# A cross-attention and FFN kernel: the output projection of a head pair as seven block products

## The reference

```
q, k, v = LN(x) @ Wq, ctx @ Wk, ctx @ Wv        # 16 heads of 128, scaled
x = x + softmax(q k^T) v @ Wo                   # Wo is 2048 x 512
x = x + down(silu(gate(n)) * up(n)), n = LN(x)  # 512 -> 2048 -> 512
```

## Time and profile before

| | us |
|---|---|
| median of 3 runs | 2033.76 (2032.74 to 2034.96) |
| the profiled execution | 2033.7 |
| its span | 2032.1 |
| PE busy | 2015.9 |
| DVE busy | 1528.7 |
| ACT busy | 1001.7 |
| POOL busy | 733.0 |

### The profile page before, as it was taken

How to read it: one execution, slowest core, us unless ns; L and a number is a source line. 1 busy time by engine, 2 the same in 40 slices (tenths; PEclk the granted TensorE clock), 3 DMA queues, 4 the chain that set the end, 5 groups by cost and what they waited for, 6 DMA issues and landing times.

```text
span 2032.1 us, 44899 instructions
## 1 busy us (share of the span) xinstructions
PE 2015.9 (99%) x15422; PEld 1509.0 (74%) x15422; DVE 1528.7 (75%) x3346; ACT 1001.7 (49%) x2679; POOL 733.0 (36%) x872
## 2 busy tenths in 40 slices
PE   8999999999999999999999999999999999999999
PEld 6888888788888887878888888888888885444444
DVE  6767777777777777777787777776666557899886
ACT  8955554554555545554555555554555443333332
POOL 5422232332333233333332323322111104877776
PEclk9999999999999999999999999999999999999999
DMA  8834444444444444444444343534332364555555
GB/s 255 217 65 90 83 97 87 84 92 92 88 88 91 92 91 86 88 89 91 89 89 92 77 105 73 104 74 91 55 82 58 68 136 97 91 89 94 92 91 99
DMA packets 456112, 193.75 MB, mean 95 GB/s; under 512 B 419456, under 2 KB 432256, under 8 KB 455904
## 3 DMA queue, kind: packets, MB, share of 16 engines
q1 hardware_dynamic: 433984, 140.31, 36.2%
q0 software_dynamic: 15584, 44.45, 8.8%
q10 hardware_dynamic: 6336, 6.29, 1.0%
HBM read 61.21 MB, written 27.26 MB: 44 GB/s over the span
## 4 chain that ended last, share of the span: by engine, by line
PE 93%; DVE 2%; DMA 2%; ACT 2%; issue 1%; DVEq 0%; SPq 0%; POOL 0%; ACTq 0%; POOLq 0%
PE b_qk L1103 33%; PE b_v L1103 17%; PE b_c L1103 10%; PE b_s L1103 9%; PE b_w L1158 8%; PE b_o L1158 8%; PE b_o L1229 3%; PE b_w L1229 2%; PE b_x L1103 2%; PE b_pt L1103 2%; DMA probT<-psplit 1%; DMA attn_weights<-wattn 0%; ACT psplit L665 0%; DVE nmax L919 0%; ACT prob L655 0%
## 5 line engine op out<-in xcount | busy, mean ns | idle before, releaser
L1103 PE MATMUL b_qk<-kvT,attn_weights 128*128 128x256 f16 x3072 | 377.2, 273 | 3.5 <-DVE qk L757 2.5
L1103 PE MATMUL b_qk<-xT,attn_weights 128*128 128x256 f16 x3072 | 377.2, 273 | 0.0
L1103 PE MATMUL b_v<-attn_weights,kvT 128*128 128x256 f16 x3072 | 377.2, 273 | 0.0
L655 ACT ACTIVATE prob<-b_s,nmax 128x256 f32<-128x256 f32 x514 | 239.2, 470 | 274.8 <-DVE nmax L919 272.8
L1103 PEld LDWEIGHTS b_qk<-kvT,attn_weights 128*128 128x128 f16 x3072 | 300.3, 98 | 92.5 <-issue 3.5
L946 DVE SCALAR_TENSOR_TENSOR psplit<-prob,rrec,psplit 128x256 f16<-128x256 f32 x514 | 307.1, 638 | 79.1 <-ACT psplit L665 79.1
L611 ACT ACTIVATE qk<-b_qk 128x512 f16<-128x512 f32 x256 | 152.5, 596 | 428.1 <-PE b_qk L1103 428.0
L757 DVE SCALAR_TENSOR_TENSOR qk<-b_qk,qk 128x512 f16<-128x512 f32 x256 | 176.7, 690 | 247.7 <-ACT qk L611 240.0
L1103 PEld LDWEIGHTS b_qk<-xT,attn_weights 128*128 128x128 f16 x3072 | 300.6, 98 | 34.8
L1103 PEld LDWEIGHTS b_v<-attn_weights,kvT 128*128 128x128 f16 x3072 | 300.6, 98 | 34.8
L665 ACT ACTIVATE psplit<-prob,rrec 128x256 f16<-128x256 f32 x514 | 233.1, 500 | 67.5 <-DVE rrec L939 67.5
(11 more groups left out here) (137 smaller groups left out, 2678.4 us busy)
## 6 DMA issues: line engine op xcount, KB each, us to landing
ffn_w<-wffn SPq DMA_DIRECT2D x48, 256.0 KB, 2.9
acc<-xtok POOLq DMA_DIRECT2D x16, 512.0 KB, 4.7
out<-acc POOLq DMA_DIRECT2D x16, 512.0 KB, 3.3
xrow<-xtok POOLq DMA_DIRECT2D x31, 256.0 KB, 3.2
kvrow<-kvt POOLq DMA_DIRECT2D x61, 128.0 KB, 2.4
out<-attn_weights POOLq DMA_DIRECT2D x28, 256.0 KB, 5.3
stage<-wattn SPq DMA_DIRECT2D x12, 512.0 KB, 4.5
ffn_scratch<-ffn_t SPq DMA_DIRECT2D x48, 128.0 KB, 1.9
```

The lines of the kernel that those rows point to most:

```text
L655: last = eng.activation(half(prob, q, 256), half(bS, q, 256), ACT.Exp, bias=nmax[:, q:q + 1], scale=1.0, accum_out=rsum[:, q:q + 1])
L1103: last = eng.matmul(out, l, r, start=(a == 0), stop=(a == len(pairs) - 1))
```

## The change

From element 2 on, the projection of a pair of heads is made by blocks. The left side is a 2 x 2 of blocks (two row tiles by two heads), the right side is a 2 x 2 (two heads by two halves of the columns). Seven products of sums of such blocks take the place of eight. Elements 0 and 1 keep the old form.

- ACT evicts contexts as float32 (`evict_rows`); POOL forms five sums in three instructions (`left_sums`); ACT writes the seven rounded blocks (`left_hi`) and DVE the remainders (`left_lo`).
- `project_fast` multiplies a pair in two steps, four terms and then three, each of three 256-column matmuls, into seven half banks (`b_pt`, `b_x`, `b_o`, `b_w`) that collect over the eight pairs. DVE adds them to `acc` in twelve additions of 256 columns (`add_products`), four in each of three steps of the next element's first quad; PE waits for them through `READ` before it opens a half bank again.
- The sums of Wo's blocks are made and split once, in element 1 (`load_out`, `out_sums`, `out_hi`, `out_sums_hi`, `out_lo`, `store_out`), and kept in DRAM. Two of eight pairs' blocks stay in SBUF, six are loaded for every element through two slots (`load_slot`), by SP, whose loop over the quads is now written out.
- The FFN weights' quantisation begins an element later, at quad 8.
- Of a tile's inverse root POOL keeps only the power (`tile_power`); DVE does the rest (`x1_aggr`, `x1_root`). Statistics move from the first quad's third and fourth step to the second quad's second.
- In the last stage the last element's twelve additions stand behind pairs 0, 1 and 2, four each; the third gate and up bank is used from chunk 6 on; the last element's other steps come ten pairs later; six pairs after the first four are without a down product, and ten halves are made behind the last pair. The buffers of the stage lie elsewhere.

```diff
-FFN_FROM, FFN_TO = QPB, QPB + FFN_TILES
+FFN_FROM, FFN_TO = 2 * QPB, 2 * QPB + FFN_TILES
...
-NO_DOWN = (0, 1, 2, 3, 36, 40, 44, 48)
+NO_DOWN = (0, 1, 2, 3, 44, 47, 50, 53, 56, 59)
...
-GU_BUF = [u % 2 if u < 4 else (u - 2) % 3 for u in range(2 * PAIRS)]
+THIRD = 6
+LAST_BEHIND = (None, None, None, 2, 1, None, 4, 6, 7, 5, 3, 10)
+GU_BUF = [u % 2 if u < THIRD else (u - THIRD + 2) % 3 for u in range(2 * PAIRS)]
...
+LEFT = {"a0": 0, "b1": 1, "a0+b1": 2, "a0+b0": 3, "a1+b1": 4, "b0-b1": 5, "a0-a1": 6}
+TERMS = (("m1", "a0+b1", 3), ("m3", "a0", 2), ("m4", "b1", 1), ("m2", "a1+b1", 0)), \
+    (("m6", "a0-a1", 5), ("m5", "a0+b0", 4), ("m7", "b0-b1", 6))
+READ = {"m1": 4, "m3": 4, "m4": 8, "m2": 8, "m6": 9, "m5": 12, "m7": 12}
...
+            def store_out(j):
+
+                eng.wait_ge(sm["wo_lo"], j + 1)
+                eng.dma_start(wos[PREP[j]], wo_split).then_inc(sm["wo_stored"], 16)
...
+            def left_sums(n, k):
+
+                wait_apart(eng, "c_hi", 4 * n + k + 1)
...
+                eng.tensor_tensor(blocks[:, 4:6, :], blocks[:, 1:9:7, :], blocks[:, 0:4:2, :], ALU.add
+                                  ).then_inc(sm["s_sum"], 1)
+                eng.tensor_tensor(blocks[:, 6:8, :], blocks[:, 0:2, :], blocks[:, 2:9:6, :], ALU.subtract
+                                  ).then_inc(sm["s_sum"], 1)
+                eng.tensor_tensor(blocks[:, 3, :], blocks[:, 1, :], blocks[:, 2, :], ALU.add).then_inc(sm["s_sum"], 1)
...
+            def left_hi(n, k):
+
+                u = 2 * n + k // 2 - 2 - FAST_PAIR
+                eng.wait_ge(sm["s_sum"], 3 * (u + 1))
...
+                eng.activation(left_part(k // 2, 0).rearrange("p (n f) -> p n f", f=P), blocks[:, 1:8, :], ACT.Copy,
+                               scale=1.0).then_inc(sm["s_hi"], 1)
...
+            def left_lo(n, k):
+
+                eng.wait_ge(sm["s_hi"], 2 * n + k // 2 - 1 - FAST_PAIR)
+                eng.tensor_tensor(left_part(k // 2, 1).rearrange("p (n f) -> p n f", f=P), blocks[:, 1:8, :],
+                                  left_part(k // 2, 0).rearrange("p (n f) -> p n f", f=P), ALU.subtract
+                                  ).then_inc(sm["s_lo"], 1)
...
+            def add_product(b, name, sign, tile_, side, behind):
+
+                if behind is not None:
+                    eng.wait_ge(sm["m_step"], 12 * (b - FAST) + behind)
+                a = acc[:, bass.ds(((b + 1) & 1) * (2 * D) + tile_ * D + side * 256, 256)]
+                eng.scalar_tensor_tensor(out=a, in0=product_at[name], scalar=sign * O_OUT, in1=a, op0=ALU.mult,
+                                         op1=ALU.add).then_inc(sm["m_step"], 1)
...
+                    sums = q == 1 and (not isinstance(s, int) or s > FAST)
+                    if sums and k > 0:
+                        add_products(s - 1, k - 1)
+                    if q == 2 and k == 1 and (not isinstance(s, int) or s > 0):
+                        for j in range(2):
+                            x1_stats(s - 1, j)
+                        x1_aggr(s - 1)
+                    if q == 2 and k == 2 and (not isinstance(s, int) or s > 0):
+                        x1_root(s - 1)
...
+                if v < 3:
+                    for at in range(4 * v, 4 * v + 4):
+                        add_last(at)
...
+                if u == THIRD:
+                    eng.wait_ge(sm["m_step"], 12 * (B - 1 - FAST) + 8)
...
+            def project_fast(u, part):
+
+                batch, first_, last_ = u // 8, u % 8 == 0, u % 8 == 7
+                slot, use = slot_use(u)
+                eng.wait_ge(sm[f"slot_loaded{slot}{part}"], 16 * use)
+                if part == 0:
+                    eng.wait_ge(sm["s_lo"], u - FAST_PAIR + 1)
...
+                for name, rows, block_ in TERMS[part]:
+                    at = LEFT[rows] * P
+                    if first_ and batch > FAST:
+                        eng.wait_ge(sm["m_step"], 12 * (batch - 1 - FAST) + READ[name])
+                    for z, (a, b) in enumerate(PARTS):
+                        last = eng.matmul(product_at[name], left_part(u % 2, a)[:, at:at + P], slot_w(slot, block_, b),
+                                          start=(first_ and z == 0 and name in OPENS), stop=(last_ and z == len(PARTS) - 1 and name in CLOSES))
+                last.then_inc(sm["o_done"], 1)
```

More of the change, by code:

```diff
@@ L260, in qk_part, with fast @@
             return qk[:, at:at + 512]
+        def fast(n, k, lead):
+            return not isinstance(n, int) or 4 * n + k - lead >= FAST_HEAD
         def head_slot(k):
@@ L337, in odd @@
-            def odd(n):
-                return (n - 1) // 2 if n % 2 and n < NQ - 4 else None
-            for n in range(QPB):
-                for k in range(QUAD):
-                    transpose_p(4 * n + k, k % 2)
-                    if n % 2 and k == 1:
-                        transpose_x(n // 2)
-                    for g in (EARLY + PIECES * n + 2 * k, EARLY + PIECES * n + 2 * k + 1):
-                        if PIECES <= g < QPB * PIECES - SLOTS:
-                            reload(g)
@@ L366, in load_x_tile @@
                                         ).then_inc(sm[f"xqT_loaded{at}"], 16)
-            for n in range(NQ - 4, NQ - 1):
-                ffn_quad(n, store=False, load=False)
-            for k in range(QUAD):
-                transpose_p(4 * (NQ - 1) + k, k % 2)
-                if k < 2:
-                    load_x_tile(k, k)
+            begin = {0: 2 * 1 + 6, 4: 2 * 3 + 6, 1: 2 * 5 + 6, 2: 2 * 6 + 6}
+            fills = {}
+            for p_, step in begin.items():
+                for part in range(2):
+                    fills.setdefault(FAST_HEAD - 16 + step + part, []).append((FAST_PAIR + p_, part, FAST_HEAD - 20 + step))
@@ new lines, in out_lo @@
+            def out_lo(j):
+                eng.wait_ge(sm["wo_hi"], 2 * j + 2)
+                to, hi_part = wo_part(1), wo_part(0)
+                pairs = [(to[:, 0:5:4, :], wo_rows[:, 0:4:3, :], hi_part[:, 0:5:4, :])]
+                for a in range(2):
+                    at = slice(1 + 4 * a, 3 + 4 * a)
+                    pairs.append((to[:, at, :], wo_sums[:, 2 * a:2 * a + 2, :], hi_part[:, at, :]))
+                pairs.append((to[:, 3, :], wo_cross, hi_part[:, 3, :]))
+                for dst, rows, above in pairs:
+                    last = eng.scalar_tensor_tensor(out=dst, in0=rows, scalar=W_SCALE, in1=above,
+                                                    op0=ALU.mult, op1=ALU.subtract)
+                last.then_inc(sm["wo_lo"], 1)
@@ L929, in quad @@
                         kv_lo(n)
-                    if ffn and k == 2:
+                    if ffn and k == 2 + sums:
                         ffn_magic(w)
@@ L1209, in _ @@
                 quad(n)
-            for n in range(FFN_FROM, NQ):
+            for n in range(QPB, NQ):
                 if n <= NQ - 4:
```

421 lines of the change are left out of this document (291 added, 130 removed).

## The result

| | before | after |
|---|---|---|
| median, us | 2033.87 (2032.74 to 2034.96, 5 runs) | 2042.87 (2042.58 to 2044.32, 5 runs) |
| the profiled execution | 2033.7 | 2043.3 |
| its span | 2032.1 | 2041.5 |

The ratio is 1.0046, with a 95% interval of 1.0031 to 1.0060: the changed kernel is 0.5% slower. 2025 us were forecast, faster; the sign is wrong, and the time lies near the upper end of the range. The granted TensorE clock was 1.000 of full speed in both kernels, so no part of the difference is the clock's.

What follows compares the result with a forecast made beforehand. TensorE, busy 99%, was taken to bound the kernel. 2033.7 - 35.7 + 15.6 + 3.5 + 4 + 1 + 5 = 2027.1, less 2 for shared stalls, gave 2025 us; range 2010 to 2044.

Steps and rivals of the forecast that it cites:

- The saving: Projection of a head pair: 21 products of 256 columns replace 12 of 512, 0.32 us for each of 112 pairs, -35.7 us.
- The boundary: First steps of the next element: PE waits for DVE's additions before reopening banks, 1.2 us per element, +15.6 us (6.5 to 29).
- Where DVE fills up: Third step of a quad: new remainder and moved root meet tile normalisation, 0.3 us stall in 11 elements, +3.5 us (0 to 14).
- the second rival: Spread stalls where DVE's new remainder meets POOL's sums or roundings: 0.15 us or more per pair turns the sign; chance 0.18.
- Element 1: Splitting the sums of Wo's blocks through one staging buffer, with store and load in turn, +4 us (0 to 16).
- Slot loads: Six of eight weight blocks reloaded for each element on SP, 672 KB every two steps, +1 us (0 to 6).
- The end: End of attention and last stage: last pairs' chain and twelve additions ahead of the first chunks, +5 us (2 to 10).
- The 2 us taken off for shared stalls: In the sum: a PE stall gives DVE back time it lacks in the next step, so 2 us were deducted.
- A chain that ends at 9.6 us: A pair's evictions, sums, blocks and remainders: DVE ends near 9.6 us, 8 us before the product, so hidden.

Runs made afterwards that it cites:

- the small remainder: The changed kernel with DVE making the remainder of one of the seven left blocks, six left out: 2022.90 us, ratio 0.9941.

## Why the prediction was wrong

- **The saving** was computed at 0.32 us per pair, 35.7 in all; measured 6.54 + 6.54 - 6.55 - 6.22 = 0.31 per pair, and some 33.4 between the step starts (the last three pairs lie behind them, in the end). The mechanism held.
- **The boundary**: forecast 1.2 us per element, 15.6; measured 0.97, 12.6. Place, wait and cause are as described (0.3 forecast for the first of the two steps, 0.32 measured); this step is right.
- **Where DVE fills up is the step that failed.** It was costed at 0.3 us in 11 elements, 3.5 us, with an upper bound of 14. Measured: 1.02 us in the 12th step and up to 0.51 in the 14th, which had no term, over 12 elements: 15.5 us, above the bound. The sum put the new remainder (1.08) and the root (0.5) on top of a qk remainder whose place was taken from the earlier trace rows, and so let the rest of DVE's row stay where it was. In fact the reciprocal came 1.25 us later against the step's start (0.42 ahead to 0.83 behind). Of that, 0.59 is the root (0.99 from 713.50 to 714.49, less 0.33 for the context remainder that went and 0.07 of small differences), near the 0.5 forecast. The other 0.66 is the row maximum, which starts 4.81 us into the step before in place of 4.13 (that step is 0.02 longer), and had no term. The prediction had read 1.58 us of idle time in that very step as DVE's room. They are gone: the moved statistics hold DVE from 707.39 to 709.25, and the qk remainder starts 4.21 us into the step in place of 3.45. The statistics aren't enough by themselves: with the small remainder, which also shortens DVE's row in the 10th step, the row maximum is at 4.13 again with the statistics where they are. No run moved them back. 1.25 + 1.0 for the remainder take the qk remainder's end from 4.84 us of the earlier trace rows to 7.09, where 6.5 was forecast. PE follows 0.15 us later, which was not counted either, in a step of 6.22. The whole stall is 1.02.
- **Contention was priced in the wrong sentence.** That POOL holds DVE's two-input remainders was seen in the earlier trace rows, and the second rival had its mechanism and its place (where the remainder meets sums or roundings), with a chance of 0.18 and a loss for each pair. The loss came only in the two steps beside the roundings: 12.7 us, against the 17 at which the rival was to turn the sign. Sums of POOL between them cost nothing that PE sees. By its own sign (waits on the qk remainder of tens of us) this rival came true in part: 20.3 us. In the trace of before the two remainders already took 2.08 us; that was paid from DVE's idle time, and the change used this up. The Trainium skill (GPSIMD Engine Reference, Key points) names the contention for instructions with two SBUF inputs; the runs agree: 2.12 us beside the roundings, 0.88 apart from them.
- **Element 1**: forecast +4, measured +4.7; the load behind the store on SP's queue is 4.0 of it by the two traces compared, 2.2 by the average of all.
- **Slot loads**: forecast +1; the waits on transposes are 1.3 us in place of 2.9. No cost, although a pair's loads are 896 KB (512 and 384 in the view of DMA issues) and not the 672 of the prediction.
- **The end**: forecast +5, measured +7.0. 5.5 of it up to the last matmul, in stalls at the places described. In size two differ: pair 127's remainder makes PE wait 1.01 (0.5 forecast), pair 126's 0.3 (0.8 forecast). The kernel after, PE:

```profile
1698.86 1.02 PE L1354 MATMUL b_s<-attn_weights,out_weights 128*128 128x512 bf16 x4 [0.57 <-ACT cbuf L770]
1703.48 0.82 PE L1415 MATMUL b_pt<-out_weights,stage 128*128 128x256 f16 x6 [1.01 <-DVE stage L1084]
1708.54 1.02 PE L1354 MATMUL b_qk<-attn_weights,out_weights 128*128 128x512 bf16 x4 [0.87 <-DVE attn_weights L987]
1713.41 1.04 PE L1354 MATMUL b_pt<-attn_weights,out_weights 128*128 128x512 bf16 x4 [1.26 <-DVE acc L1107]
1719.84 1.04 PE L1354 MATMUL b_pt<-attn_weights,out_weights 128*128 128x512 bf16 x4 [1.08 <-DVE attn_weights L987]
```

  They answer to the one 0.83 of the earlier trace rows. The other 1.5 us are behind the last matmul, and were not forecast: the last stores take longer to land. The views of DMA issues of before and of after (count, KB, median us to landing):

```profile
out<-acc SPq DMA_DIRECT2D x4, 256.0 KB, 3.2
```

```profile
out<-acc SPq DMA_DIRECT2D x4, 256.0 KB, 4.8
```

  Why they do was not tried, and stays open, as do some 2 of the 5.5 us: 1.9 are the additions, 0.8 go with the root and 0.6 with the remainder.
- **The 2 us taken off for shared stalls** had no row behind it. The stalls lie in different steps and add up.
- **Two slips that change nothing.** A chain that ends at 9.6 us ends 3.15 us before the end of the next step (6.54 + 6.21 = 12.75), not 2.4; and 4.84 + 1.08 + 0.5 is 6.4, not 6.5.

The forecast with the measured terms: 12.0 more in the third quad, 2.3 less saved, 2.0 more at the end, the 2.0 not taken off, 0.7 each in elements 1 and 0, 2.3 of rest, 3.0 less at the boundary and 1.0 less for loads are 18 us; 2025 becomes 2043.

## What to carry to other kernels

When work is added to an engine that runs two or more of its streams in one order, lay out its whole row again from the step before, not only the instruction that is late; a gap in the old row can be spent once, and contention that the gap used to pay for becomes the stall. Where two engines hold each other up, first ask whether the one without a deadline can wait: one added wait on POOL gave 12.7 us, three ways of moving DVE's work gave some 3 us at best. In a step with a tight bank, put deferred reads as early as the data is complete, even if that makes the groups uneven.

## What the runs showed of the hardware

- The hold-up between DVE and POOL goes both ways. POOL's clip of 512 columns (0.62 us in the kernel before, 0.63 where it waits for the x_norm) took 1.56 when DVE's 896-column remainder started with it. DVE's 1.08 did not grow in this meeting.
- DVE's instructions that read PSUM did not stretch beside POOL: the qk remainder 0.68, the row maximum 0.68 and an addition 0.41 in every timeline shown. In the whole trace of the kernel after no row maximum and no qk remainder took over 0.69 us, though some four or five of ten ran beside POOL's instructions. A small tensor_scalar with both sides in SBUF did: `rsum`, two columns, takes 0.16 at 715.28 and 1.03 in this line of the kernel after, beside POOL's 1.27 and 1.26:

```profile
168.93 1.03 DVE L1179 TENSOR_SCALAR rsum<-rsum 128x2 f32<-128x2 f32 x1 [2.75 <-ACT prob L816]
```

- Products of 256 columns in place of 512 cost TensorE next to nothing here: a step with twelve of them took 6.55 us, and 6.54 with six of 512.
